# Sparse layer: masks with the group's row outermost, compares on ScalarE, every dot product beside the first product

## The reference

```python
x = x + xattn(layernorm(x), ctx)          # 16 x 100 tokens of 1024, 32 heads of 128, 4 kv heads
xf = layernorm(x)
inter = xf @ c1_w.T @ c2_w.T              # rank 16, 3584 gate values a token
blk = inter.reshape(tokens, 56, 64)
idx = argmax(blk, axis=-1) + arange(0, 3584, 64)     # one row in each group of 64
h = relu(einsum('bkm,bm->bk', w1[idx], xf))
x = x + einsum('bk,bkm->bm', h, w2t[idx])
```

## Time and profile before

| | |
|---|---|
| median of 3 runs | 3539.28 us (3535.36 to 3540.3) |
| profiled execution, its own time | 3539.46 us |
| span of its profile | 3537.8 us |
| TensorE matmul / weight load busy | 3419.9 us (97%) / 3044.1 us (86%) |
| VectorE / ScalarE / GpSimd busy | 2248.0 us (64%) / 1372.0 us (39%) / 877.6 us (25%) |
| `second_norm_and_gates` | 2562.8 to 2605.2 us |
| `hidden_layer` | 2605.2 to 3103.7 us |
| `project_down` | 3108.8 us to the end |

### The profile page before, as it was taken

The page is one execution under the profiler, slowest core; times in us unless marked ns, Lnnn a source line. Parts: engine busy times, 40 slices in busy tenths (PEclk is TensorE's granted clock), DMA queues, the critical chain, the costliest instruction groups (busy, mean ns, idle before and its releaser), DMA issues. The chain is left out here.

```text
span 3537.8 us, 51963 instructions
## 1 busy us (share of the span) xinstructions
PE 3419.9 (97%) x18422; PEld 3044.1 (86%) x18422; DVE 2248.0 (64%) x3746; ACT 1372.0 (39%) x2610; POOL 877.6 (25%) x1108
## 2 busy tenths in 40 slices
PE   6999999799999999999999899999989999999999
PEld 5888888699999899999999778788789999977877
DVE  5555567677866577777777523433277787766775
ACT  4333344344433577777777422322231111121120
POOL 0000000000000477777776100000011111144543
PEclk8999999899999999999999999999999999999999
DMA  3333332354444334444333654544334444589786
GB/s 119 106 97 104 96 108 84 96 141 125 118 117 124 109 106 112 111 113 113 107 94 87 193 126 121 178 130 120 106 125 149 153 166 156 172 314 310 259 292 215
DMA packets 477970, 501.72 MB, mean 142 GB/s; under 512 B 172580, under 2 KB 372260, under 8 KB 477764
## 3 DMA queue, kind: packets, MB, share of 16 engines
q1 hardware_dynamic: 441988, 371.79, 36.0%
q0 software_dynamic: 34720, 125.19, 10.2%
q10 hardware_dynamic: 1056, 2.10, 0.2%
HBM read 383.98 MB, written 115.02 MB: 141 GB/s over the span
## 5 line engine op out<-in xcount | busy, mean ns | idle before, releaser
L2087 PE MATMUL wo_acc<-wo_w,wo_l 128*128 128x512 f32 (+1 forms) x2496 | 577.4, 393 | 17.0 <-DVE wo_l L2037 16.9
L269 PE MATMUL kv_bank<-kv_wo,kv_so 128*128 128x512 f32 x2436 | 575.0, 395 | 15.4 <-DVE kv_wo L361 11.1
L2087 PEld LDWEIGHTS wo_acc<-wo_w,wo_l 128*128 128x128 f32 (+1 forms) x2496 | 462.1, 186 | 132.2 <-DVE wo_w L2061 16.9
L269 PEld LDWEIGHTS kv_bank<-kv_wo,kv_so 128*128 128x128 f32 x2436 | 457.9, 190 | 110.4 <-issue 16.7
L657 PE MATMUL pr_bank<-pr_xo,pr_wp 128*128 128x400 f32 x2688 | 498.7, 347 | 29.0 <-ACT pr_s L724 13.4
L657 PEld LDWEIGHTS pr_bank<-pr_xo,pr_wp 128*128 128x128 f32 x2688 | 493.5, 190 | 31.8 <-DVE pr_wp L741 24.0
L1698 PE MATMUL hid_acc<-x1t,hid_w 128*128 128x336 f32 x2688 | 440.0, 319 | 0.0
L2376 PE MATMUL w_acc<-w_w,w_l 128*128 128x512 f32 (+1 forms) x1848 | 421.3, 390 | 5.2 <-DVE w_l L2315 5.2
L1698 PEld LDWEIGHTS hid_acc<-x1t,hid_w 128*128 128x128 f32 x2688 | 415.7, 189 | 1.1
L2376 PEld LDWEIGHTS w_acc<-w_w,w_l 128*128 128x128 f32 (+1 forms) x1848 | 339.0, 184 | 87.1 <-DVE w_l L2315 5.3
L2037 DVE TENSOR_TENSOR wo_l<-wo_l_raw,wo_l 128x512 fp32r<-128x512 f32 (+1 forms) x208 | 139.3, 671 | 344.5 <-ACT wo_l L2010 344.3
(11 more groups left out here) (194 smaller groups left out, 4581.0 us busy)
## 6 DMA issues: line engine op xcount, KB each, us to landing
wo_l_raw<-o_scratch SPq DMA_DIRECT2D x192, 256.0 KB, 2.9
pair_raw<-in_L_xattn_Wq_dram SPq DMA_DIRECT2D x64, 512.0 KB, 6.0
q_scratch<-pr_out SPq DMA_DIRECT2D x128, 200.0 KB, 2.6
o_scratch<-o_stage SPq DMA_DIRECT2D x64, 400.0 KB, 3.7
q_raw<-q_scratch SPq DMA_DIRECT2D x64, 384.0 KB, 3.1
stage<-in_ctx_dram SPq DMA_DIRECT2D x45, 512.0 KB, 4.0
h_scratch<-c_raw SPq DMA_DIRECT2D x28, 672.0 KB, 3.2
wo_w_raw<-in_L_xattn_Wo_dram SPq DMA_DIRECT2D x16, 1024.0 KB, 7.0
```

The source lines that it names most:

```text
L269: last = pe.matmul(bank[:, BANK[i], :], so[:, i, a, c, :], wo[:, i, e, c, :], start=(not opened and c == 0 and (a, e) == PAIRS[0]), stop=( ...
L2087: last = pe.matmul(acc[p][:rows, :], l[j % 2][:, a, k, :rows], w[:, c, m * per + k, :], start=(m == 0 and k == 0 and (a, c) == PAIRS[0]), ...
```

## The change

It has four parts.

1. **Masks.** The layout is `` with the tiles innermost, instead of the rows of the group. Tiles are held in two halves: x = 0 for the first eight, x = 1 for the other five (`spans` 16 and 10: two groups a tile). VectorE only makes the largest value (`largest`, negated), once for each of the four groups of tiles. ScalarE compares: `signs` issues one ACTIVATE (Sign, with the negated largest as bias) for each 64 values, 16 for four tiles and 4 for one. Then VectorE makes for each half of the tiles a `tree`: `keyed` adds the key (in bf16, from a table `key_bf` that is now 64 x 16 instead of 64), `halved` and `quartered` take maxima of halves, `leading` the maximum over the last 16, `mark` the mask. `masked` counts 2 for a pair instead of 4. `close` reads its mask as stationary operand with a step of 16 or 10 elements.
2. **Order.** ScalarE's and VectorE's orders in the hidden layer are written anew around this.
3. **Dot products.** All 112 are in `hidden_layer`, 8 or 9 in each pair but the first, over a ring of 5 rows. `project_down` has the accumulations alone. `R_HIDDEN, R_DOWN, SUMS = 5, 5, 0`; SUMS = 0 means that no accumulation is moved.
4. **Memory.** The running totals of the sparse tiles have their own place (`totals`), lent as two of the rows' buffers to the stage ahead, and loaded with the residual at the start of `hidden_layer`. The high and low parts of the sparse tiles' tokens go to a temporary `x1s`, so that `x1t` holds the dense tokens alone; for this `zg` becomes `(0, 2), (2, 6), (6, 9), (9, 13)`.

```diff
-    zg = [(0, 4), (4, 7), (7, 10), (10, NT)]
+    S = len(keep)
+    zg = [(0, S), (S, S + 4), (S + 4, S + 7), (S + 7, NT)]
...
-            pool.tensor_copy(key_bf[:, :], keys[:, :]).then_inc(made, 1)
+            pool.tensor_scalar(key_bf[:, :, :], keys[:, :].rearrange("q (c a) -> q c a", a=1).to_broadcast(
+                [P, sparsity, most]), 1.0 / P, None, ALU.mult).then_inc(made, 1)
...
             def close(m, p, t):
                 for x, (k, n, a, b, lo, hi) in enumerate(parts[t]):
-                    at = k * per + p * (per // 2)
-                    last = pe.matmul(acc[:, t, lo:hi], mask[m][:n, at:at + per // 2, :].rearrange("q a b -> q (a b)"),
+                    x_half, at = divmod(2 * k + p, spans[0])
+                    last = pe.matmul(acc[:, t, lo:hi], mask[m][x_half][:n, :, :, at].rearrange("q a b -> q (a b)"),
                                      closed[:n, a:b], start=False, stop=(x == len(parts[t]) - 1))
...
-                        pe.wait_ge(masked, NP)
+                        pe.wait_ge(masked, 2)
...
+            def signs(i, k):
+                a, n = picks[k]
+                x_half, at = divmod(2 * a, spans[0])
+                act.wait_ge(topped, NP * i + k + 1)
+                if not isinstance(i, int) or i > 0:
+                    act.wait_ge(masked, 2 * (i - 1) + k // 2 + 1)
+                values = gate[:, :, :].rearrange("q a (b c) -> q (a b) c", c=sparsity)
+                for x in range(n * per):
+                    last = act.activation(equal[x_half][:, x % pair, :, at + x // pair], values[:, x, :], ACT.Sign,
+                                          bias=top[:, a * per + x:a * per + x + 1])
+                last.then_inc(compared, 1)
...
             def body(i, m, more, first):            # ScalarE
+                    if early:
+                        for k in range(NP):
+                            signs(0, k)
...
+                    evacuate(i, p, 0)
+                    if late:
+                        signs(1, 1)
+                    if another:
+                        high_part(j + 1, 1 - p, 0)
+                    if more and not late:
+                        signs(i + 1, 2 * p)
+                    evacuate(i, p, 1)
+                    if late:
+                        signs(1, 2)
+                    if another:
+                        high_part(j + 1, 1 - p, 1)
+                    evacuate(i, p, 2)
+                    if more:
+                        signs(i + 1, 2 * p + 1)
+                    evacuate(i, p, 3)
...
+            def tree(i, m, x, between):             # VectorE
+                keyed(i, x)
+                steps(between[:1])
+                halved(i, x)
+                quartered(i, x)
+                steps(between[1:2])
+                leading(i, x)
+                steps(between[2:3])
+                mark(i, m, x)
+                if x == 0:
+                    indices(i)
+
+            def first_pair():
+                for x in range(2):
+                    largest(0, 2 * x)
+                    largest(0, 2 * x + 1)
+                    tree(0, 0, x, ())
+                low_part(1, 1, 0)
+                low_part(1, 1, 1)
+                largest(1, 0)
+                largest(1, 1)
+                low_part(2, 0, 0)
+                largest(1, 2)
+                low_part(2, 0, 1)
+                tree(1, 1, 0, ())
+                largest(1, 3)
+                tree(1, 1, 1, ())
+
+            def body(i, m, more):
+                mine = list(sparse.body[i])
+                cuts = (0, 1, 2, 5, 6, 6, len(mine)) if more else (0, 2, 4, 6, 8, 8, len(mine))
+                a, b, c, d, e, f = [mine[cuts[n]:cuts[n + 1]] for n in range(6)]
+                low_part(2 * i + 1, 1, 0)
+                if more:
+                    largest(i + 1, 0)
+                steps(a)
+                low_part(2 * i + 1, 1, 1)
+                steps(b)
+                if more:
+                    largest(i + 1, 1)
+                steps(c)
+                if more:
+                    low_part(2 * i + 2, 0, 0)
+                    largest(i + 1, 2)
+                    tree(i + 1, 1 - m, 0, d)
+                    low_part(2 * i + 2, 0, 1)
+                    steps(e)
+                    largest(i + 1, 3)
+                    tree(i + 1, 1 - m, 1, f)
+                    steps(f[3:])
+                else:
+                    steps(d + e + f)
+                clip(i)
```

More of the change, by code:

```diff
@@ L1517, in __init__, with earlier @@
         sums = [("out", n % S, n // S) for n in range(S * groups)]
[L1518 to L1526, removed]
+        bodies = groups // per - 1
+        self.hidden, self.body = [], [range(0)]
+        for b in range(bodies):
+            first = len(self.hidden)
+            mine = dots[len(dots) * b // bodies:len(dots) * (b + 1) // bodies]
+            assert mine[-1][2] // per <= b + 1
+            self.hidden += mine
+            if b:
+                self.hidden += sums[self.SUMS * (b - 1):self.SUMS * b]
+            self.body.append(range(first, len(self.hidden)))
+        self.down = sums[self.SUMS * (bodies - 1):]
+    def earlier(self, steps, k):
+        return max([j for j in range(k) if steps[j][:2] == steps[k][:2]], default=None)
     def gather(self, pool, kind, s, g, row):
@@ L1565, in hidden_layer @@
     NP = len(picks)
+    assert NP == 4
+    pair = per // 2
+    spans = [sum(n for _, n in picks[2 * x:2 * x + 2]) * 2 for x in range(2)]
+    most = max(spans)
     parts = [[] for _ in range(tiles)]
@@ L1631, in _ @@
             store(blocks - 2, 0)
-            sp.wait_ge(dotted, len(sparse.hidden) - 2)
+            sp.wait_ge(dotted, max(lent) + 1)
             for p in range(2):
@@ new lines, in sparse_step, with clip @@
+                if kind == "in":
+                    sparse.dot(dve, s, g, ring[k % slots]).then_inc(dotted, 1)
+                else:
+                    before = sparse.earlier(sparse.hidden, k)
+                    if before is None:
+                        dve.wait_ge(totals_in, 16 * sparse.S)
+                    else:
+                        dve.wait_ge(dotted, before + 1)
+                    sparse.axpy(dve, s, g, ring[k % slots], sparse.totals[s]).then_inc(dotted, 1)
+            def clip(i):
+                mine = [k for k in sparse.body[i] if sparse.hidden[k][0] == "in"]
+                dve.wait_ge(dotted, mine[-1] + 1)
+                sparse.clip(dve, [sparse.hidden[k] for k in mine]).then_inc(clipped, 1)
@@ new lines, in steps @@
+            def steps(some):
+                for k in some:
+                    sparse_step(k)
+            def tree(i, m, x, between):
[24 more added lines that the diff above has]
+                tree(1, 1, 1, ())
```

219 lines of the change are left out of this document (94 added, 125 removed).

## The result

The changed kernel takes 3576.05 us (median of 4 runs, 3573.92 to 3578.27) beside 3539.4 us for the kernel before on the same chip: ratio 1.0105, 95% interval 1.0092 to 1.0118. It is 36.7 us slower. Forecast were 3565 us, slower, range 3546 to 3596: direction and range hold, and the sum of the parts, 25.6 us, is 11 us short.

A forecast was written before the change was run, and what follows sets the result against it. The prediction took TensorE to bound the kernel, so relieving VectorE buys almost nothing and later masks cost time. Its terms summed to 25.6 us more than the profiled 3539.46, giving 3565 us, range 3546 to 3596.

The forecast's parts named there:

- Rival 5: Down product: its matmuls run faster once gathers and dots leave, up to 27 us back, 3522 us; chance 0.04.
- First block: Hidden layer's block 0: fourth gates wait for compares behind the x=0 tree, +7.2 us; slower clock afterwards, +2.
- Second block: Hidden layer's block 1: gates come late as compares and largest run without a spare bank, +3 us together.
- Its masks: Second block's closes: masks end at 30.2 us while TensorE asks at 27.2, +3 us.
- Steady pairs: Later pairs of the hidden layer: masks 0.7 us late in seven of twelve bodies, those with 9 dots, +5 us.
- Loads of the masks: Closes: 392 weight loads read strided instead of packed bf16 columns, 10 ns more each, +4 us.
- Rival 1: Closes: strided mask loads at the fp32 pace or worse, at 50 ns each 3582 us; chance 0.15.
- Key table: Start of the hidden layer: VectorE's first split waits for GpSimd's larger key table, +0.4 us.
- The stage ahead: Second norm and gates: new tile groups make the last product 448 columns instead of 320, +1 us.
- Rival 2: Hidden layer: only the start late, compares at 0.21 us, loads free, +9 to +14, 3551 us; chance 0.12.
- rival 4: Whole kernel: nothing measurable, first pair's waits hidden, within 7 us, 3542 us; chance 0.08.
- Rival 3: All twelve pairs: masks late by about 1.5 us, from a table switch or slower chain, 3582 us; chance 0.09.

The follow-up runs named there:

- b_dots8: Kernel before with 8 instead of 6 dot products in each pair, 104 of 112 in the hidden layer, old mask chain: 3538.68 us, ratio 1.0.
- a_order: Changed kernel with VectorE making the largest of group 2 ahead of the first tree in the first pair: 3573.09 us, ratio 1.01.
- a_packed_act: Changed kernel with compares written packed and the last maximum read packed, masks and row numbers then wrong: 3562.22 us in one run.
- a_marks_first: Changed kernel with the dot products behind the mark in every tree, not between its steps: 3568.73 us in one run.
- b_step16: Kernel before with each close reading its 128 mask columns at a step of 16 elements (32 bytes), entries wrong: 3548.44 us, ratio 1.0027.

## Why the prediction was right, and where it was short

The direction and the mechanism came as forecast: TensorE was at its limit, so relief of VectorE was worth nothing, and what was lost is waiting at the places named. The sum was 11 us short, nearly all of it in terms that were sized too low: the mask loads (6 us and more), the second block (3), the first (2) and the key table (1.6). The range held because its high end had 20 us for the loads.

- **TensorE is the bound, relief of VectorE buys nothing.** Right: b_dots8 measured 1.0, and the down product is 429.0 us in both profiles, with 45 us less VectorE work in it (250.5 us busy instead of 295.3). Rival 5 (a faster pace of the down product) falls: 1848 matmuls took 421.3 us in both.
- **First block, +7.2 and +2 for the clock.** Right in place and mechanism; a_order showed that the tree in front of the largest made 4 of the 6.6 us. Measured +10.9. From the first to the fourth gates it is 9.3 more where I had 7.2, and the short term is the compare: 16 took 4.6 to 4.8 us where I took 4.0, for three groups one after the other, and the first group's, which I had in time, made TensorE wait 0.39. The tree was well sized as a whole, 4.96 us for 4.8, but by errors that cancel: its last maximum took 1.19 where I took 0.69, the row numbers and the hand-over between steps less than I had. I had both as bounds: a compare of 0.31 at most, and a strided maximum at half speed (+0.5, it is +0.48). a_packed_act shows that both come from the step alone. I took the low end for the maximum on the reason that the other operands are packed, and that was no reason. Behind the fourth gates it is 1.6 more. The 24 sums there lost 1.8 us at the lower clock, but the masks were ready only 0.9 us before TensorE closed (2642.44 and 2643.30), so about 1 us of it shows; a_order, with the clock up, needed 1.0 less from the fourth gates to the closes.
- **Second block, +3, measured +6.3.** Waits of 1.9, 0.6 and 2.1 us (3.7 more than before) in place of 3, plus 1.6 us of slow clock behind the first of them, which I had counted only for block 0, and about 1 us that was not taken apart, part of it longer closes. Its masks, +3: 2.7.
- **Steady pairs, +5, measured +4.2.** Right in mechanism, which a_marks_first shows: seven waits, as many as there are bodies with 9 dots and a tree, 0.6 us each where I had 0.7. The masks' slower steps had their share in it (a_packed_act).
- **Loads of the masks, +4.** The term that was mis-sized most in us: a pair of blocks in the middle takes 35.85 us instead of 35.10, over 10 us in all, and b_step16 gives as much without the rest of the change. I took 10 ns a load for hiding beside matmuls; about 27 of the 56 ns more are seen. In the kernel before this row comes one pair, 35.10 us, after that at 2895.29; in the changed kernel the two rows at 2889.86 and 2925.71 above are a pair apart:

```profile
2930.39 3.95 PE L1698 MATMUL hid_acc<-x1t,hid_w 128*128 128x336 f32 x24
```

  Rival 1 had the place right and the size (50 ns) too large, and my sign, closes 50 to 60 ns apart, was that of the kernel before (14 closes in 0.90 us); now 14 take 1.15. SBUF — State Buffer of the Trainium skill (Specifications, Cachelines) foretold a penalty, and the runs agree: 98 ns packed, 155 at 16 bytes and more. It asks for two hits a line for full bandwidth; with two columns in 16 bytes the load still took 120 ns, and there the measurement decides. TensorE: Matmul & The Clock Gate of the Trainium skill (Weight-path perf modes), which admits packed or strided columns, doesn't say that they are equally fast. I had read that into it, and they aren't.
- **Key table, +0.4, measured +2.0.** One TENSOR_SCALAR of 1024 elements took 1.18 us, this one 2.79. The row had one source packed and in place; this reads a column of keys 16 times over and writes bf16. Which of the two makes it slow was not tried.
- **The stage ahead, +1.** -0.6 between these two profiles, but that is scatter: the nine profiles with the new groups have 41.9 to 43.6 us, 42.9 in the mean, and the five with the old ones 40.7 to 42.4, 41.6 in the mean. The difference of the means, 1.3, fits the forecast.
- **The other rivals.** Rival 2 (only the start is late, quick compares, free loads) and rival 4 (nothing measurable) fall with the compares' time, the loads and the 36.7 us. Rival 3 (a table switch at compares) did not come: no ACT_TABLE_LOAD stands among them, and of the steady pairs' masks seven are late, not all.

With these sizes blocks 2 to 27 are accounted for: 10 us of loads and 4.2 of late masks make the 14.0 of the table. What stays open is why the clock falls behind some waits of 2 to 3 us and not behind others of the same length, and even behind the same pause in one profile and not in another.

## What to carry to other kernels

When the bound engine is already at 100%, judge a change to a helper engine by latency, not by busy time: find what the bound engine asks for and count the whole order that stands in front of the answer, here a tree of 5 us in front of a maximum of 1.2. The long step of this layout made three of its users pay, each in its own way (the weight load, ScalarE's write, VectorE's last maximum), so cost each reader and writer at the step, above all a stationary operand that is loaded next to short matmuls. A start-up increment behind a slow instruction on a side engine is a wait in disguise.

## What the runs showed of the hardware

- Mask loads of 128 bf16 columns: 98 ns packed, 120 at a step of 8 bytes, 156 at 16 and 155 at 32; with steps of 32 and 20 bytes mixed 154. Between the short matmuls of the closes 27 or 28 of the 56 ns more are seen in TensorE's time.
- ScalarE, 64 values from PSUM with a pointer bias: 213 ns in a row when the bf16 output is packed, 305 when its step is 32 or 20 bytes.
- VectorE's maximum over 512 bf16 values: 686 ns packed, 1165 at a step of 32 bytes, over 320 values 481 packed and 783 at 20 bytes. By the two lengths that is about 2 ns an element instead of 1.
- VectorE's bf16 `tensor_tensor` of 2048 elements: 1.22 us with a packed output, 9.5 us with an output step of 256 bytes. This was by far the largest surprise: 4.6 ns an element. Whether the write or the length of the step makes it so much dearer than the steps of 20 and 32 bytes above was not tried.
- The clock behind a pause: with the same code and the same pause the first 24 sums of the layer took 5.96 us in one profile (before) and 3.85 in another (b_dots8).
